# Half of one depthwise tap on TensorE by diagonal weights, three whole taps for the first 18 tiles, and two sum buffers for GpSimd

## What is computed

```python
# layer 0
x = x + conv0(group_norm(x))                    # a bilinear shift per channel, a scale, a 1x1 convolution
# layer 1
h = concat(haar_dwt(group_norm(x)))             # 4*128 channels at 128 x 128
h = gelu(batchnorm(conv1x1(h, w_c1, b_c1)))     # 128 channels; the norm runs over the whole batch
res = h
o = dwconv3x3(h, dw_w, dw_b)                    # nine taps per channel
o = layernorm_chw(o, gn_g, gn_b)                # one mean and variance per image
o = conv1x1(o, pw1_w, pw1_b); o = gelu(o); o = conv1x1(o, pw2_w, pw2_b)
h = o + res
h = gelu(batchnorm(conv1x1(h, w_c2, b_c2)))     # 4*128 channels, whole batch again
x = x + haar_idwt(h)
```

## Time and profile before

| | |
|---|---|
| median of 3 runs | 5600.16 us |
| the profiled execution | 5600.85 us, its span 5599.2 us |
| busy over the span | PE 4595.8 us, DVE 4814.4, ACT 4173.9, POOL 1109.0 |
| DVE's add_tap L1206 | 640 times, 781.5 us busy, 1272 ns each |
| POOL's tap multiplication L406 | 256 times, 1117 ns each |

### The profile page before, as it was taken

One profiled execution on the slowest core, in us unless ns is written; L12 is line 12 of the kernel. 1 busy time (PEld: TensorE's weight loads), 2 busy tenths in 40 slices (PEclk: granted clock), 3 DMA queues, 4 the chain that ended last, 5 costly groups with the idle time before them and its releaser, 6 DMA issues.

```text
span 5599.2 us, 54191 instructions
## 1 busy us (share of the span) xinstructions
PE 4595.8 (82%) x12292; PEld 2113.4 (38%) x12292; DVE 4814.4 (86%) x4445; ACT 4173.9 (75%) x5706; POOL 1109.0 (20%) x779
## 2 busy tenths in 40 slices
PE   1889999999999999999952777777897777777775
PEld 0334444444444444444421444444552222222222
DVE  6998898988989889899649999999738888888887
ACT  4887777777777777777536777777648888888887
POOL 0000000000000000000038777777601111111111
PEclk6999999999999999999976999999999999999998
DMA  8999999999999999999962333333239999999999
GB/s 337 371 361 412 426 425 426 417 426 425 417 426 417 426 420 421 424 360 396 348 221 79 117 117 118 119 117 117 99 100 236 235 236 236 236 236 236 236 236 224
DMA packets 260905, 1627.49 MB, mean 291 GB/s; under 512 B 30768, under 2 KB 31152, under 8 KB 96944
## 3 DMA queue, kind: packets, MB, share of 16 engines
q1 hardware_dynamic: 168624, 1022.13, 46.0%
q0 software_dynamic: 36864, 268.45, 23.1%
q10 hardware_dynamic: 55296, 335.57, 14.3%
HBM read 954.94 MB, written 671.09 MB: 290 GB/s over the span
## 4 chain that ended last, share of the span: by engine, by line
PE 35%; DMA 23%; DVE 16%; POOL 11%; issue 8%; ACT 3%; DVEq 0%; POOLq 0%; ACTq 0%; SPq 0%
DMA out_x<-arena 19%; PE ps L742 13%; PE ps L730 10%; PE ps L725 9%; POOL arena L420 5%; POOL arena L425 4%; DMA arena<-in_x 4%; DVE arena L1093 3%; DVE arena L1217 2%; DVE arena L1079 2%; ACT arena L687 2%; POOL arena L406 2%; DVE arena L1108 2%; DVE ps L1206 2%; DVE arena L972 1%
## 5 line engine op out<-in xcount | busy, mean ns | idle before, releaser
L897 PE MATMUL ps<-arena,c2T 128*128 128x512 f32 x2048 | 1035.6, 658 | 379.7 <-ACT arena L680 368.6
L730 PE MATMUL ps<-arena 128*128 128x512 f32 x2048 | 965.5, 595 | 24.9 <-DVE arena L1108 24.9
L742 PE MATMUL ps<-arena 128*128 128x512 f32 x2048 | 965.0, 615 | 12.3 <-DVE small L1057 10.4
L725 PE MATMUL ps<-arena 128*128 128x512 f32 x1920 | 913.8, 598 | 43.1 <-DVE arena L1028 22.7
L406 POOL TENSOR_SCALAR arena<-arena,taps 128x1024 f32<-128x1024 f32 (+1 forms) x256 | 285.9, 1117 | 2922.8 <-ACT arena L598 2891.5
L478 ACT ACTIVATE arena<-ps,small 128x1024 f32<-128x1024 f32 x512 | 568.1, 1109 | 322.1 <-PE ps L730 321.8
L680 ACT ACTIVATE arena<-ps,small 128x512 f32<-128x512 f32 x1024 | 713.5, 778 | 105.7 <-DVE arena L1322 94.5
L1206 DVE SCALAR_TENSOR_TENSOR ps<-arena,taps,ps 128x1024 f32<-128x1024 f32 (+1 forms) x640 | 781.5, 1272 | 6.5 <-ACT ps L624 5.8
L897 PEld LDWEIGHTS ps<-arena,c2T 128*128 128x128 f32 x2048 | 406.2, 207 | 1008.3 <-ACT arena L680 562.1
L1079 DVE SCALAR_TENSOR_TENSOR arena<-arena,shift 128x2048 f32<-128x2048 f32 x256 | 601.3, 2349 | 201.1 <-DMA arena<-in_x 139.2
L456 ACT ACTIVATE ps<-arena 128x1024 f32<-128x1024 f32 x512 | 526.3, 1028 | 169.4 <-ACT arena L478 159.5
(11 more groups left out here) (160 smaller groups left out, 5242.3 us busy)
## 6 DMA issues: line engine op xcount, KB each, us to landing
arena<-in_x SPq DMA_DIRECT2D x400, 1024.0 KB, 15.9
out_x<-arena ACTq DMA_DIRECT2D x256, 1024.0 KB, 9.0
arena<-out_x SPq DMA_DIRECT2D x256, 1024.0 KB, 16.9
out_x<-arena POOLq DMA_DIRECT2D x256, 1024.0 KB, 17.0
arena<-in_x SPq DMA_DIRECT2D x112, 1152.0 KB, 15.5
y_dram<-arena ACTq DMA_DIRECT2D x128, 512.0 KB, 8.6
arena<-y_dram SPq DMA_DIRECT2D x128, 512.0 KB, 3.2
h_dram<-arena SPq DMA_DIRECT2D x128, 512.0 KB, 2.6
```

What stands on the lines that cost most here:

```text
L725: mm(ps[:, r, :], w_right[:, :], u_buf[k][:, 2 * r:2 * r + 2, 2:W + 2], start=False, stop=False, skip_group_check=True)
L730: last = mm(ps[:, r, :], w_center[:, :], v_buf[k][:, r * BANK:(r + 1) * BANK], start=False, stop=True, skip_group_check=True)
L742: last = mm(ps[:, 4 + s % 2, :], w_c1b[:, q, :], cells[:, q // 2, q % 2, :, :], start=(q == 0), stop=(q == 3))
L897: last = mm(ps[:, 4 * k + q, :], c2T[:, q, :], h2_in[s // 2][:, k * HC:(k + 1) * HC], start=True, stop=True)
```

## The change

PE takes over taps by products with diagonal matrices, which add onto what `put_tap` wrote. In tiles 0 to 17 (`HEAD` = 18) PE adds the three taps (0,0), (0,1), (0,2), each in two products of 4 rows, DVE adds the three taps of the lower row, and POOL has two taps left (one by itself, one by ACT) in place of three. From tile 18 on PE adds tap (0,1) for the upper four rows of the tile, and DVE the same tap for the lower four. PE's taps come last in its step; DVE's first tap of a tile waits for them in place of put_tap. In the head one tap of tile s-1 is early (`early(t)`) instead of three. POOL's sum has two buffers and waits for finish_o of the tile before the last one. ACT makes the product of tile s-1 right after make_h(s), and squares tile s-3 instead of s-2, but for the last tile of an image. Four banks are filled once by PE before the middle part, and the first two put_tap wait for that. Sizes of buffers and the helper `pool_done`, which counts POOL's operations, are left out here.

```diff
+PE_TAP = (0, 1)
+PE_ROWS = TROWS // 2
-DVE_TAPS = [(0, 1), (0, 2), (2, 0), (2, 1), (2, 2)]
+DVE_TAPS = [(0, 2), (0, 1), (2, 0), (2, 1), (2, 2)]
 EARLY = 3
+HEAD = 18
+HEAD_PE_TAPS = [(0, 0), (0, 1), (0, 2)]
...
-        pool_a, pool_b, pool_sum = (cut(TILE) for _ in range(3))
+        pool_a, pool_b = (cut(TILE) for _ in range(2))
+        pool_sum = [cut(TILE) for _ in range(2)]
...
+        def pe_taps(t):
+            return [(tap, half) for tap in HEAD_PE_TAPS for half in range(2)] if t < HEAD else [(PE_TAP, 0)]
+        def pool_taps(t):
+            return POOL_TAPS[:2] if t < HEAD else POOL_TAPS
+        def dve_taps(t):
+            if t < HEAD:
+                return [(tap, 0) for tap in DVE_TAPS if tap not in HEAD_PE_TAPS]
+            return [(tap, PE_ROWS if tap == PE_TAP else 0) for tap in DVE_TAPS]
+        def early(t):
+            return 1 if t < HEAD else EARLY
...
         def tap_order(s):
-            late = [(s - 2, i) for i in range(EARLY, len(DVE_TAPS) + 1)]
-            early = [(s - 1, i) for i in range(EARLY)]
-            return [(t, i) for pair in zip(late, early) for t, i in pair if 0 <= t < TILES]
+            late = [(s - 2, i) for i in range(early(s - 2), len(dve_taps(s - 2)) + 1)]
+            soon = [(s - 1, i) for i in range(early(s - 1))]
+            pairs = itertools.zip_longest(late, soon)
+            return [op for pair in pairs for op in pair if op and 0 <= op[0] < TILES]
...
-                if t:
-                    pool.wait_ge(dw_acc, o_made(t - 1))
+                if t >= 2:
+                    pool.wait_ge(dw_acc, o_made(t - 2))
                 pool.wait_ge(pool_step, n + 1)
-                pool.tensor_tensor(pool_sum, pool_a, pool_b, ALU.add).then_inc(pool_step, 1)
+                pool.tensor_tensor(pool_sum[t % 2], pool_a, pool_b, ALU.add).then_inc(pool_step, 1)
+                if len(pool_taps(t)) > 2:
...
             def put_tap(t):
                 act.wait_ge(h_ready, nth(t))
+                if t < 2:
+                    act.wait_ge(primed, 2)
...
             def make_product(t):
                 if t:
-                    act.wait_ge(pool_step, (t - 1) * POOL_OPS + 2)
+                    act.wait_ge(pool_step, pool_done(t - 2) + 2)
...
                 if s < TILES:
                     make_h(s)
+                if 0 <= s - 1 < TILES:
+                    make_product(s - 1)
                 if 0 <= q < TILES:
                     make_a(q)
+                if 0 <= s - 3 < TILES and (s - 3) % NT != NT - 1:
+                    square_o(s - 3)
...
-                if s < TILES:
-                    make_product(s)
-                if 0 <= s - 2 < TILES:
+                if 0 <= s - 2 < TILES and (s - 2) % NT == NT - 1:
                     square_o(s - 2)
...
+            def add_pe_taps(t):
+                pe.wait_ge(dw_put, nth(t))
+                for tap, half in pe_taps(t):
+                    rows_ = h_tile(t, *tap, 4 * half, 4 * half + 4)
+                    first = max(0, top(t, tap[0]) - 4 * half) * HW
+                    last = mm(ps[:, 4 + 2 * (t % 2) + half, first:], tap_diag[:, HEAD_PE_TAPS.index(tap), :], rows_,
+                              start=False, stop=True, skip_group_check=True)
+                last.then_inc(pe_tapped, 1)
             pe.wait_ge(bn1_ready, 1)
+            for bank in range(4, 8):
+                last = prime(bank)
+            last.then_inc(primed, 1)
             for s in range(TILES + OLD_LAG + 2):
...
                 if 1 <= q <= TILES:
                     turn_h2(q - 1, 1)
                     gram_half(q - 1, 0)
+                if s < TILES:
+                    add_pe_taps(s)
...
+            for n, tap in enumerate(HEAD_PE_TAPS):
+                ts(tap_diag[:, n, :], ident[:, :], tap_weight(*tap), None, ALU.mult)
...
-                dy, dx = DVE_TAPS[i]
+                (dy, dx), first = dve_taps(t)[i]
                 if i == 0:
-                    dve.wait_ge(dw_put, nth(t))
+                    dve.wait_ge(pe_tapped, t + 1)
...
-                acc = dw(t)[:, top(t, dy):end(t, dy), :]
-                stt(out=acc, in0=h_tile(t, dy, dx), scalar=tap_weight(dy, dx), in1=acc,
+                acc = dw(t)[:, max(first, top(t, dy)):end(t, dy), :]
+                stt(out=acc, in0=h_tile(t, dy, dx, first), scalar=tap_weight(dy, dx), in1=acc,
                     op0=ALU.mult, op1=ALU.add).then_inc(dw_acc, 1)
```

More of the change, by code:

```diff
@@ L1 @@
+import itertools
 from contextlib import ExitStack
@@ L62, in preact_kernel @@
         taps = sb("taps", [P, 9])
+        tap_diag = sb("tap_diag", [P, len(HEAD_PE_TAPS), P])
         bdw = sb("bdw", [P, 1])
@@ L96, in preact_kernel @@
         gram = sb("gram", [P, P + 1])
-        arena = sb("arena", [P, 49300])
+        arena = sb("arena", [P, 50300])
         at = [0]
@@ L103, in cut @@
             at[0] += n
-            assert at[0] <= 49300
+            assert at[0] <= 50300
             return arena[:, at[0] - n:at[0]]
@@ L169, in end, with h_tile, pool_ops, pool_done @@
             return TROWS - 1 if dy == 2 and t % NT == NT - 1 else TROWS
-        def h_tile(t, dy=1, dx=1):
+        def h_tile(t, dy=1, dx=1, first=0, last=TROWS):
             r = 1 + t % RING * TROWS + dy - 1
-            return h_rows[:, r + top(t, dy):r + end(t, dy), dx:dx + HW]
+            return h_rows[:, r + max(first, top(t, dy)):r + min(last, end(t, dy)), dx:dx + HW]
+        def pe_taps(t):
+            return [(tap, half) for tap in HEAD_PE_TAPS for half in range(2)] if t < HEAD else [(PE_TAP, 0)]
+        def pool_taps(t):
+            return POOL_TAPS[:2] if t < HEAD else POOL_TAPS
+        def pool_ops(t):
+            return 2 * len(pool_taps(t)) - 2
+        def pool_done(t):
+            return sum(pool_ops(k) for k in range(t + 1))
+        def dve_taps(t):
[4 more added lines that the diff above has]
+            return 1 if t < HEAD else EARLY
         def tap_weight(dy, dx):
@@ L190, in o_made @@
         def o_made(t):
-            return TAP_COUNT[t, len(DVE_TAPS)]
+            return TAP_COUNT[t, len(dve_taps(t))]
         def norm_step(s):
             return (s - NT - 2) // NT if s >= NT + 2 and (s - 2) % NT == 0 and s < TILES + NT else None
-        POOL_OPS = 2 * len(POOL_TAPS) - 2
         def banks(half):
@@ L236, in preact_kernel @@
         pool_step, w_ready, product_made = sem("pool_step"), sem("w_ready"), sem("product_made")
+        pe_tapped = sem("pe_tapped")
         pw1_done, a_ready, pw2_done, h2_ready = sem("pw1_done"), sem("a_ready"), sem("pw2_done"), sem("h2_ready")
@@ L409, in _ @@
             for t in range(TILES):
-                n = t * POOL_OPS
+                n = pool_done(t - 1)
                 pool.wait_ge(h_ready, nth(t))
@@ L415, in _ @@
                 pool.wait_ge(product_made, t + 1)
-                if t:
-                    pool.wait_ge(dw_acc, o_made(t - 1))
+                if t >= 2:
+                    pool.wait_ge(dw_acc, o_made(t - 2))
                 pool.wait_ge(pool_step, n + 1)
-                pool.tensor_tensor(pool_sum, pool_a, pool_b, ALU.add).then_inc(pool_step, 1)
[L421 to L426, removed]
+                pool.tensor_tensor(pool_sum[t % 2], pool_a, pool_b, ALU.add).then_inc(pool_step, 1)
+                if len(pool_taps(t)) > 2:
+                    pool.wait_ge(pool_step, n + 2)
+                    pool_tap(pool_a, t, POOL_TAPS[2])
+                    pool.wait_ge(pool_step, n + 3)
+                    first, last = top(t, POOL_TAPS[2][0]) * HW, end(t, POOL_TAPS[2][0]) * HW
+                    total = pool_sum[t % 2][:, first:last]
+                    pool.tensor_tensor(total, total, pool_a[:, first:last], ALU.add).then_inc(pool_step, 1)
             with pool.Fori(0, B) as b:
@@ L1204, in add_tap @@
                     dve.wait_ge(h_ready, nth(t + 1))
-                acc = dw(t)[:, top(t, dy):end(t, dy), :]
-                stt(out=acc, in0=h_tile(t, dy, dx), scalar=tap_weight(dy, dx), in1=acc,
+                acc = dw(t)[:, max(first, top(t, dy)):end(t, dy), :]
+                stt(out=acc, in0=h_tile(t, dy, dx, first), scalar=tap_weight(dy, dx), in1=acc,
                     op0=ALU.mult, op1=ALU.add).then_inc(dw_acc, 1)
             def finish_o(t):
-                dve.wait_ge(dw_acc, TAP_COUNT[t, len(DVE_TAPS) - 1])
-                dve.wait_ge(pool_step, (t + 1) * POOL_OPS)
+                dve.wait_ge(dw_acc, TAP_COUNT[t, len(dve_taps(t)) - 1])
+                dve.wait_ge(pool_step, pool_done(t))
                 if t >= RING:
@@ L1216, in finish_o @@
                     dve.wait_ge(hT_done, nth(q * 2 + 1))
-                stt(out=o_ring[t % RING], in0=flat(dw(t)), scalar=1.0, in1=pool_sum, op0=ALU.mult, op1=ALU.add,
+                stt(out=o_ring[t % RING], in0=flat(dw(t)), scalar=1.0, in1=pool_sum[t % 2], op0=ALU.mult, op1=ALU.add,
                     accum_out=sums_o[:, 0, t % NT:t % NT + 1]).then_inc(dw_acc, 1)
@@ L1264, in _ @@
                 for n, (t, i) in enumerate(tap_order(s)):
```

(2 more changed lines are left out.)

## The result

The changed kernel takes 5590.37 us, median of 22 runs (5586.81 to 5594.45), against 5599.7 us for the kernel before in the same jobs (22 runs, 5596.94 to 5605.24): ratio 0.9984, 95% interval 0.9977 to 0.9990. That is 9 us faster, where 28 us slower was predicted. The profiled span is 5587.7 us against 5599.2, 11.5 less.

The account below looks back on a forecast made before the run. DVE's own instruction stream was taken to bound the steady steps. Head +87, steady steps -59 and setup +0.5 gave +28 us on 5600.85, or 5629, stated as 5628 us; 8 in 10 range 5597 to 5672.

Parts of the forecast that it names:

- DVE's stream bounds the steady step, and the half tap takes 0.54 us off.: Tiles 18 to 127: DVE's instructions fill the 8.29 us step; the half tap makes it 7.75, in all -59 us.
- Rival (c): Steady steps: PE binds, the step stays at 8.0 to 8.3 us, total 5656 to 5687 us; chance 0.13.
- The head becomes a serial chain through put_tap, PE's burst and DVE.: Tiles 0 to 17: a new chain makes each turn 13.0 us against 7.50; the head's sum is +87 us.
- the first finish_o: Start of the head: finish_o of tile 0 comes at about 2907.1 in place of 2901.37, +5.7 us.
- The clock falls before nearly every burst and is back 5 us into it.: Head: PE's clock falls in the 5.1 us idle time, returns after 5.05 us in the mean; burst 7.9 us.
- Rival (a): Head: PE's clock stays up, turn 10.5 us, sum -12, total 5589 us; chance 0.11.
- Rival (e): Head: PE's burst is hidden behind DVE, step 4.7 or 5.4 us, total 5508 us; chance 0.02.
- The later norm steps: Norms after the first: DVE's shorter wait for square_o and the extra PE product cancel; 0, from -8 to +10 us.
- the extra PE product shifts the following steps: Later norms: the added product falls at half clock and delays following steps by as much as the up to 1 us gained.
- The two sum buffers: POOL no longer waits for finish_o.: Steady steps: POOL needs 7.4 us and, with two sum buffers, no longer waits for finish_o of the tile before.
- one DVE tap fewer: Head, the turn after the one with the first image's norm: DVE has a tap fewer, -1.5 us.

Follow-up runs that it names:

- e_nohead: The changed kernel without its head (HEAD = 0), tiles 0 to 17 shared out like all others: 5503.36 us, ratio to before 0.9827.
- e_filler: The changed kernel with five more PE products after each head tile's taps, their results never used: 5553.43 us, ratio 0.9916.
- e_hold: The kernel before with one wait added: POOL's third tap in one tile per norm waits for the norm's weights: 5570.94 us, ratio 0.9949.
- e_actorder: The kernel before with ACT's new order alone and one sum buffer: 5595.72 us, ratio 0.9992.
- e_headorder: The changed kernel with the last taps and finish_o of tile s-1 put ahead of the head tap that waits for PE's burst: 5476.51 us, ratio 0.9781.

## Why the prediction was wrong

By its own steps:

- *DVE's stream bounds the steady step, and the half tap takes 0.54 us off.* Right: 8.29 to 7.76 us, -58.7 us of a predicted -59. The 512 form takes 759 ns, 532 less than the 1291 of the 1024 form. Rival (c) fell: PE at 49.52 of 50, more than the 96% of the prediction's sum, with no DVE wait for it.
- *The head becomes a serial chain through put_tap, PE's burst and DVE.* Right: 12 instructions behind 5.05 us of idle time, and the turn's mean is 12.80 us against 13.0 (12.97 over a full cycle of five). Turns run 11.90, 12.77, 13.20, 13.44, 13.54 and again 11.90, as the clock's changes shift against the bursts. With the first finish_o the head came to +84.9 of +88.2, and e_nohead, against a head with half taps, shows 87 us for the whole of it.
- *The clock falls before nearly every burst and is back 5 us into it.* Right: a mean burst of 12.80 - 5.05 = 7.75 us (predicted 7.9; single bursts run from 6.85 to 8.49), and e_filler gives the other level, 5.42. In the trace the granted clock falls 0.5 to 2.2 us before a burst begins and is back 2.9 to 6.2 us into it, 5.07 in the mean over five turns. Rival (a) would have given 5589 us, which is the time measured, but its turn of 10.5 us at clock 1.00 is not what the trace shows. The right number here stands for the wrong mechanism. What the clock cost in all, 37 us, is 0.7% of the kernel: that it is small beside the kernel did not make the turn 10.5 us.
- *Rival (e): the head could not be hidden, by the order of DVE's instructions.* Right for this kernel, and the reason was the order alone: with finish_o moved ahead the turn is 5.97 us with the same two dw buffers. (The rival's 5508 us left out the later first finish_o; with its +5.7 the prediction's own terms give 5515.)
- ***The later norm steps: "I take 0, from -8 to +10."* This is the step that failed.** They gave -30.4 us, and in the first norm held operations were worth 3.5 us more, by e_hold. The prediction took the norm's small operations at what they take and asked only what DVE waits for. It saw half of the mechanism: the wait for the squares, worth 11.4 us over eight norms, which e_actorder alone turned into some 5 us, with no gain still inside its interval. It did not see that DVE was busy where it should have been waiting: 1604 ns for a 128x1 operation that takes 160 stands in the busy time, and no view of waits names it. The bound of -8 was made from the wait alone, at "up to 1 us" for each norm, so it was no bound. Of the 39 us between the predicted +28 and the -11 of the trace, these are 30.4; the first norm gives 5.6 and the head 3.3. The offset, "the extra PE product shifts the following steps", is real and small: the third step lasts 0.62 us longer.
- *The two sum buffers: POOL no longer waits for finish_o.* Right and incomplete: the prediction counted POOL's freedom as free. By itself it costs 15 us; with ACT's order it is part of a gain of 46.

The first step of a later norm, -3.0 us, can be added up as well. Before, in order of time:

```profile
3163.62 2.08 POOL L425 TENSOR_TENSOR arena<-arena 128x896 f32<-128x896 f32 x1
3164.75 0.19 DVE L1233 TENSOR_REDUCE small<-sums_o 128x2 f32<-128x32 f32 x1 [2.09 <-ACT arena L641]
3164.97 0.76 DVE L1234 TENSOR_SCALAR small<-small 128x2 f32<-128x2 f32 x1
...
3165.88 1.12 POOL L406 TENSOR_SCALAR arena<-arena,taps 128x1024 f32<-128x1024 f32 x1 [0.17 <-ACT arena L598]
3166.02 0.98 DVE L1238 TENSOR_TENSOR small<-small,bdw 128x1 f32<-128x1 f32 x1
```

And after:

```profile
3233.66 0.19 DVE L1288 TENSOR_REDUCE small<-sums_o 128x2 f32<-128x32 f32 x1 [0.41 <-ACT arena L677]
3233.88 0.17 DVE L1289 TENSOR_SCALAR small<-small 128x2 f32<-128x2 f32 x1
```

In this norm the wait for the squares falls from 2.09 to 0.41 us (-1.7), L1234 and L1238 are freed (0.76 to 0.17 and 0.98 to 0.16, -1.4), L1291 is held (+0.9), the half tap saves 0.5, and two short waits of 0.2 together go.

The 5.5 us in the first norm's step from 16 to 17 split into 3.5 for held operations (e_hold) and 2.0 for the rest, where the prediction had 1.5 for one DVE tap fewer. Open is why the third step of a norm varies so much (8.85 to 10.13 us in the changed kernel).

## What to carry to other kernels

Before pricing an edit of the order, list DVE's smallest operations by form with their mean ns. Free, the 128x1 operations here took 0.15 to 0.22 us by kind; those with a mean of several times that were held by POOL, and any edit that moves POOL can free or hold them, so the range must include the whole of that surplus (here 35 us in the five groups named above, their means less what they take when free). Where a chain of small DVE operations stands on the critical path, keep POOL out of all of it, even by an added wait. An engine that takes over work must be fed from the front of the other's queue: the instruction that frees its next input goes ahead of the one that waits for its result.

## What the runs showed of the hardware

Some small DVE operations whose operands lie in SBUF end with the POOL instruction that was running when they began, whether that was a 1.12 us TENSOR_SCALAR or a 2.35 us TENSOR_TENSOR. Counted over the middle part in all twelve profiles, for operations that began at least 0.03 us after POOL's did and 0.4 us before its end, 164 of 165 ended within 0.1 us of it: all 65 TENSOR_TENSOR and 45 SCALAR_TENSOR_TENSOR of 128x1, 34 of 35 TENSOR_SCALAR of 128x2, and all 20 TENSOR_SCALAR of 128x128. Others were not held at all: 102 TENSOR_SCALAR of 128x1 took their 153 to 156 ns inside a POOL instruction, 29 TENSOR_REDUCE 185 to 188 ns and 3 RECIPROCAL 154 ns. Two of them in the changed kernel:

```profile
3238.27 1.12 POOL L438 TENSOR_SCALAR arena<-arena,taps 128x1024 f32<-128x1024 f32 x1
3238.36 0.15 DVE L1065 TENSOR_SCALAR small<-small 128x1 f32<-128x1 f32 x1
3238.55 0.15 DVE L1066 TENSOR_SCALAR small<-small 128x1 f32<-128x1 f32 x1
```

DVE's taps, which read one operand in PSUM, keep their 1281 to 1291 ns beside a POOL that is busy 40 us of 50. The Trainium skill (SBUF — State Buffer, SBUF: two separate sides) states that DVE and GpSimd share a port pair as an exclusive lock for a whole instruction, for DVE operations with two SBUF inputs or in a two-port mode. The trace agrees for the operations with two SBUF inputs (0.16 against 2.22 us) and for the taps. L1234 (128x2) and L1246 (128x128) have one tensor input and were held too, where the same kind at 128x1 was not; the second of the two cases would fit them, but no run here shows the mode.

The clock: in the head of the changed kernel, with 5.05 us of idle time ahead of each burst of 12 instructions (six products), it stood at 0.77 to 0.79 on average; in e_filler, with the idle time filled down to 0.76 us, and in e_headorder, with 1.36 us, it stood at 1.00. Products whose results are thrown away paid back 37 us of 5590.
